# The last head's first maxima put into the first eight of its twelve expert tiles, with group 0's negative maxima made and sent before the last two tiles end

## What is computed

```python
x = L0_attn_hidden_states                      # 2 x 1024 x 256
xn = _layernorm(x)
x = x + attention(xn) + experts(xn)

# attention, per sequence and head
scores = q @ k.T * scale + slope * (pos_k - pos_q)     # causal, else -1e9
attn = softmax(scores, axis=-1)
out = (attn @ v) @ out_w.T + out_b

# experts
scores = sigmoid(x @ gate_w); selected = top_k(scores + expert_bias, 2)
routed += comb[:, e] * (silu(g) * u @ experts_down[e])  # for each expert e
shared = silu(x @ shared_gate_w) * (x @ shared_up_w) @ shared_down_w
```

## Time and profile before

| | |
|---|---|
| median of three runs | 511.94 us (509.26 to 513.58) |
| the profiled execution | 515.17 us, span 513.3 us |
| TensorE matmul busy | 449.6 us, 88% of the span |
| VectorE | 334.2 us, 65% |
| ScalarE | 249.0 us, 49% |
| GpSimd | 155.8 us, 30% |
| chain that ended last | TensorE 72%, VectorE 13%, DMA 7% |

### The profile page before, as it was taken

The page is one execution under the profiler, slowest core; times in us unless marked ns, Lnnn a source line. Parts: engine busy times, 40 slices in busy tenths (PEclk is TensorE's granted clock), DMA queues, the critical chain, the costliest instruction groups (busy, mean ns, idle before and its releaser), DMA issues.

```text
span 513.3 us, 8621 instructions
## 1 busy us (share of the span) xinstructions
PE 449.6 (88%) x2987; PEld 259.9 (51%) x2988; DVE 334.2 (65%) x621; ACT 249.0 (49%) x567; POOL 155.8 (30%) x178
## 2 busy tenths in 40 slices
PE   4597764498899999995998999999999999999996
PEld 3446652386576666673534444344444444433454
DVE  3869940365366666665786767867688586874667
ACT  2630520331333333331766667676676676766730
POOL 2380777201500000004888888840000101000000
PEclk9699795599999999997899999999999999999999
DMA  8797972379999984334116519162080000001103
GB/s 270 148 402 266 349 269 102 112 240 270 184 226 222 226 189 123 115 100 145 49 42 127 100 50 179 39 108 41 13 132 1 5 1 5 1 2 15 34 32 102
DMA packets 51484, 64.64 MB, mean 126 GB/s; under 512 B 13810, under 2 KB 44674, under 8 KB 49878
## 3 DMA queue, kind: packets, MB, share of 16 engines
q1 hardware_dynamic: 47046, 55.20, 41.8%
q0 software_dynamic: 3296, 8.52, 6.1%
q10 hardware_dynamic: 1104, 0.41, 0.3%
HBM read 37.47 MB, written 27.13 MB: 126 GB/s over the span
## 4 chain that ended last, share of the span: by engine, by line
PE 72%; DVE 13%; DMA 7%; issue 5%; SPq 2%; ACT 1%; DVEq 0%
PE ps L1277 12%; PE ps L1072 11%; PE ps L1251 10%; PE ps L1263 10%; PE ps L1176 9%; DVE mx L987 5%; PE ps L1192 5%; PE ps L1266 2%; PE ps L1252 2%; PE ps L1166 2%; DMA qs<-nr 2%; DMA x_in<-sorted_tokens 2%; DMA x_sb<-x 2%; PE ps L1205 2%; PE ps L1122 1%
## 5 line engine op out<-in xcount | busy, mean ns | idle before, releaser
L735 ACT ACTIVATE pt<-ps 128x512 f32<-128x512 f32 (+3 forms) x384 | 167.2, 491 | 83.7 <-PE ps L1266 47.7
L987 DVE TENSOR_REDUCE mx<-ps 128x1 f32<-128x384 f32 (+6 forms) x189 | 153.8, 863 | 55.8 <-PE ps L1252 53.2
L1277 PE MATMUL ps<-pt,vg 128*32 128x512 f32 (+3 forms) x768 | 71.9, 492 | 0.0
L592 POOL DMA_INDIRECT yg<-sorted_outputs,slot_i x32 | 32.7, 1020 | 109.5 <-DMA sorted_outputs<-y_out 101.0
L1263 PE MATMUL ps<-qs,ks 111*128 111x512 bf16 (+3 forms) x192 | 56.3, 333 | 4.1 <-DMA qs<-nr 3.3
L1176 PE MATMUL ps<-w_gu,hx 128*128 x192 | 54.2, 407 | 4.0 <-issue 3.3
L1263 PE MATMUL ps<-qk 111*128 111x512 bf16 (+3 forms) x192 | 54.6, 328 | 2.5 <-DMA qk<-nr 1.3
L1251 PE MATMUL ps<-qk 108*128 108x512 bf16 (+3 forms) x192 | 50.2, 328 | 2.8 <-DVE mx L987 2.4
L1266 PE MATMUL ps<-cbf 128*128 128x128 bf16 x256 | 52.6, 222 | 0.0
L1252 PE MATMUL ps<-cbf 128*128 128x128 bf16 x224 | 47.6, 225 | 0.0
L952 DVE COPY y_out<-ps 128x256 f32<-128x256 f32 x48 | 20.4, 424 | 37.7 <-PE ps L1192 37.6
(11 more groups left out here) (176 smaller groups left out, 680.1 us busy)
## 6 DMA issues: line engine op xcount, KB each, us to landing
sorted_tokens<-y_out SPq DMA_DIRECT2D x12, 512.0 KB, 5.0
qk_parts<-parts SPq DMA_DIRECT2D x16, 384.0 KB
x_in<-sorted_tokens SPq DMA_DIRECT2D x48, 128.0 KB, 4.0
sorted_outputs<-y_out SPq DMA_DIRECT2D x48, 128.0 KB, 2.1
qk<-qk_parts SPq DMA_DIRECT2D x8, 384.0 KB
w_gu<-e_gu SPq DMA_DIRECT2D x1, 2816.0 KB
x_sb<-x SPq DMA_DIRECT2D x4, 512.0 KB, 9.2
w_dn<-e_dn SPq DMA_DIRECT2D x1, 2048.0 KB, 8.3
```

The lines of the kernel that those rows point to most:

```text
L592: g_.indirect_dma_start(out=yg[:, n % 4, :], out_offset=None, in_=ysd, in_offset=bass.IndirectOffsetOnAxis(ap=slot_i[:, k, t:t + 1], axis= ...
L735: sc.activation(pt[:, s % 4, j, lo:CH], bank(n % 3)[:, lo:CH], ACT.Exp).then_inc(s_exp, 1)
L987: last = v.reduce_max(dst, src, axis=AX.X)
L1277: ins = te.matmul(ps[32 * j:32 * j + 32, OUT_BANK * CH + lo:(OUT_BANK + 1) * CH], vg[:, par, kb, j, :], pt[:, s % 4, j, lo:CH], start=kb = ...
```

## The change

The fourth head's eight maxima follow its tiles 0 to 7 (overall tiles 36 to 43) in place of 0, 2, 3, 5, 6, 8, 9 and 11. After its tile 9 (overall 45) TensorE transposes the maxima and VectorE makes the negative ones, and SyncE sends them after the store of tile 45, ahead of the stores of tiles 46 and 47. In the kernel before, all three steps come after tile 47. VectorE's helper functions also change place in the file, which moves line numbers alone. The waits added are those that the moved steps carry: TensorE's for the 32 maxima (s_ff) after tile 45, and SyncE's for the finished parts (s_n) ahead of store 46.

```diff
 FIRST_HEAD_AT = [NTH - QT + q for q in range(QT)]
+LAST_HEAD_AT = list(range(QT))
+FIRST_NEG_AT = QT + 1
...
             for k in range(NT - 8, NT):
                 store_tile(k, k % 4)
-            store_neg(0, 0)
+                if k == NT - NTH + FIRST_NEG_AT:
+                    store_neg(0, 0)
...
             def tile_steps(j, first, last):
...
                     tile_step(k + u, u % 4, NTH - u if last else NT, None if first and u < 4 else stored)
                     for q in range(QT):
-                        if (FIRST_HEAD_AT if first else FIRST_AT)[q] == u:
+                        if (FIRST_HEAD_AT if first else LAST_HEAD_AT if last else FIRST_AT)[q] == u:
                             first_maxima(j, q, j * QT + q)
+                    if last and u == FIRST_NEG_AT:
+                        negate(0, 0, first=True)
...
-            negate(0, 0, first=True)
             for p in range(EARLY):
                 maxima(1, 1, p)
...
                     for q in range(QT):
-                        if (FIRST_HEAD_AT if first else FIRST_AT)[q] == u:
+                        if (FIRST_HEAD_AT if first else LAST_HEAD_AT if last else FIRST_AT)[q] == u:
                             first_scores(j, q, j * QT + q, first)
+                    if last and u == FIRST_NEG_AT:
+                        pe.wait_ge(s_ff, HG * QT)
+                        te.transpose(bank(6, P, HG * QT), mx[:, 0, :], ident[:, :]).then_inc(s_fr, 1)
...
             tile_steps(HG - 1, False, True)
-            pe.wait_ge(s_ff, HG * QT)
-            te.transpose(bank(6, P, HG * QT), mx[:, 0, :], ident[:, :]).then_inc(s_fr, 1)
             pe.wait_ge(s_yo, NT)
             pe.wait_ge(s_ff, HG * QT + 1)
```

More of the change, by code:

```diff
@@ L937, in _, with negate @@
                 add_shared(n)
+            def negate(g, par, first=False):
+                ready, freed, n = (s_fr, s_ff, HG * QT) if first else (s_mxr, s_mxf, g * NP - 1)
+                dve.wait_ge(ready, n + 1)
+                src = bank(6, P, HG * QT)
+                v.tensor_scalar(nr[:, par, 0, :], src, -1.0, None, ALU.mult).then_inc(s_nstep, 1)
+                dve.wait_ge(s_nstep, g * 2 + 1)
+                v.scalar_tensor_tensor(nrf[:, par, :], src, -1.0, nr[:, par, 0, :], ALU.mult,
+                                       ALU.subtract).then_inc(freed, 1)
+                dve.wait_ge(freed, n + 1 if first else MX_CREDIT + n + 1)
+                v.tensor_copy(nr[:, par, 1, :], nrf[:, par, :]).then_inc(s_nstep, 1)
+                dve.wait_ge(s_nstep, g * 2 + 2)
+                v.tensor_tensor(nr[:, par, 2, :], nrf[:, par, :], nr[:, par, 1, :], ALU.subtract).then_inc(s_n, 1)
             def tile_hidden(k, w):
@@ L988, in maxima @@
                 last.then_inc(s_mxf, 1)
[L990 to L1002, removed]
             def beside(g, par, ahead):
```

## The result

The changed kernel takes 1.0058 times as long as the kernel before, with a 95% interval of 1.0037 to 1.0079. That is 3.0 us more (1.9 to 4.1); the medians of eight runs are 516.30 and 512.03 us, 4.3 us apart, and the text goes by the ratio. The forecast was 0.35% slower, 1.8 us, in a range of 509.7 to 516.5 us; the measured median lies inside it, 0.2 us from its upper end. The interval is clear of no change, which the prediction had not expected of so small a difference.

The account below looks back on a forecast made before the run. TensorE ran at full clock in most slices, except around the 7.6 us tail before group 0, mostly latency. Group 3's start (-0.2) and half clock (+2.0) gave +1.8 us: 517.0 profiled, 513.7 on the median, range 509.7 to 516.5.

Parts of the forecast that it names:

- The tiles: Tiles 36 to 45, sized from the first head's tiles with maxima blocks: tile 45 starts at 229.18 us, 0.65 late.
- The negative maxima: Between tile 45 and group 0: parts ready at about 233.1 us in place of 236.62, group 0 3.6 us earlier.
- The landing: From the first issue of the three DMAs to TensorE's start of group 0: 4.81 us, unchanged.
- The clock at group 0: TensorE's clock no longer falls to half at group 0's start, as the tail is filled: 2.03 us back.
- SyncE's order: The three DMAs go ahead of the last two stores, so GpSimd's first gather moves 1.52 us later, to 237.93.
- The wait at group 3: TensorE, 5.6 us ahead, waits 5.4 us for GpSimd's v copy ending at 338.60; 0.2 us of gain is left.
- GpSimd's own stretch: GpSimd's work from the first gather to the end of group 3's v copy: 100.67 us, taken as unchanged.
- The half clock behind the wait: TensorE's work after the wait at group 3 starts at half clock: 2.0 us lost, between 0 and 4.1.
- The sum: Whole kernel: -0.2 us at group 3's start and +2.0 of half clock make +1.8 us, 0.35% slower.
- The v copy does not bind: Rival, chance 0.12: GpSimd has more slack at group 3, the whole 5.6 us stays, 506.3 us, 1.1% faster.
- Binds, but the clock does not fall: Rival, chance 0.18: TensorE waits for the v copy at group 3 without half clock; only -0.2 us, 511.7 us.
- A long cold start: Rival, chance 0.08: half clock lasts much longer after the wait at group 3, 20 us giving +7.6, 519.5 us.

Follow-up runs that it names:

- the maxima alone: Changed kernel with transposition, negation and sending put back behind tile 47, only the fourth head's maxima kept early; 0.9980 (0.9955 to 1.0005) of the kernel before.

## Why the prediction was right, point by point

**The tiles.** Foreseen from tile 36 to tile 45: 18.43 us. Measured: 225.67 - 207.10 = 18.57. The first head's rows were the right stand-in.

**The negative maxima.** Foreseen 22.35 us from tile 36 to ready parts, measured 229.57 - 207.10 = 22.47. The landing was mis-sized: 4.81 us from the first issue was taken from the kernel before, and it took 232.89 - 229.60 = 3.29. With the parts 0.1 later, that put group 0 a further 1.4 us ahead, all of which went into the wait. The 4.81 was not a chance of one execution: in the kernel before with GpSimd 4 us longer it took 4.76, and with the maxima alone 4.73; with the early v copy in the kernel before it took 3.97 (issue 233.72, group 0 at 237.69). The six kernels that send early took 3.14 to 3.85. So the way from issue to group 0 mostly became shorter with the change, where the prediction had it unchanged; why, no run shows.

**The clock at group 0.** Foreseen +2.0 back, measured 8.25 - 6.23 = 2.0. That it came out to the tenth is luck: in four of the six executions with the early sending the clock fell here all the same, though none of these kernels alters TensorE's work up to there (GpSimd 4 us longer: 7.49 us). The mean of the six is 6.81 us and that of the three of the kernel before 7.91, a gain of 1.1. In the changed kernel's time this hardly counts, since the wait at group 3 takes up what group 0 gains or loses.

**SyncE's order.** Foreseen 1.52 us later for the first gather, measured 27.87 - 25.66 = 2.21. Of the 0.7 us between, 0.4 is the issue of the last two stores: 1.06 us together (0.5 each), where 0.32 to 0.36 each had been put in, taken from the last store of the kernel before. The other 0.3 is the three rows: ready 0.1 later, and 1.99 us to issue in place of 1.84.

**The wait at group 3.** Foreseen 5.4 us, measured 7.55. The 2.15 us more are four terms, to within 0.1: group 0 began 1.4 us earlier than thought, TensorE's way from there to group 3 took 94.55 us in place of 333.2 - 237.9 = 95.3, the gather came 0.7 us later, and against these GpSimd's own stretch was 0.75 us shorter. Foreseen start 0.2 us earlier than before, measured 0.19 from tile 36. This agreement is luck, since two errors met: the gather came 0.7 us later than thought, and GpSimd's own stretch took 99.92 us in place of 100.67, since two waits of 0.7 us for gathered rows fell to one of 0.55.

**The half clock behind the wait.** Foreseen 2.0 us, measured 1.73, and shown as a cost of its own by the kernel that kept TensorE busy (13.51 us back to 11.78). The rule of the Trainium skill (TensorE: Matmul & The Clock Gate, section on oscillation) holds here: the trace has 7.55 us of idle time and then 4.44 us at clock 0.50.

**The sum.** +1.8 foreseen, and from the two profiled executions, both from tile 36 on: 511.7 - 207.10 = 304.6 against 513.3 - 210.75 = 302.55, +2.05. The ratio says +3.0 (1.9 to 4.1). The rest, if it is not noise, may lie in the kernel before: its profiled execution reached group 3 1.4 us later (128.08) than the one with the early v copy (126.65), which does the same work up to there and runs in the same time. Against that one the sum is 1.24 + 1.73 = 3.0. The kernel that keeps TensorE busy points the same way: without the half clock it is still 1.5 us (0.4 to 2.6) slower than the kernel before, where the prediction has -0.2. I took one execution's distance to group 3 as the kernel's, and its slack of 1.75 us with it. That the loss at group 3 is a microsecond more is worked out from one execution of each kernel, not shown.

**The rivals.** "The v copy does not bind" is refuted by the 7.55 us; what it would have given, 1.1% faster, is what the variant with the early copy gave (1.0%). "Binds, but the clock does not fall" is refuted for the changed kernel by the 4.44 us at 0.50; the kernel with TensorE kept busy is that case made, though at +1.5 us and not at the -0.2 that the rival gave. A long cold start did not come: the clock was back after 4.44 us.

## What to carry to other kernels

When a stage is shortened, look down the program for every place where another engine joins, and read its slack there: what reaches the stage behind it can't be more than the slack there (1.75 us here by one execution, less what the change itself adds to that engine's start, 1.5 foreseen and 2.2 measured). Read the slack in more than one execution: here one had 1.75 us and another about 1. What is moved ahead in an in-order queue pushes back what it passes; ask who waits for that, even 100 us later. Each idle wait of TensorE at group 3 cost more than its length, 1.1 to 2.2 us more, because the work behind it ran at half clock, and the remedy may be one line elsewhere: moving a 0.6 us copy turned +0.6% into -1.0%.

## What was not expected of the hardware

- From the first issue of the same three small DMAs to TensorE's start of group 0 it took 3.14 to 3.85 us in the six kernels that send early, and 3.97 to 4.81 in the four that send behind tile 47 and negate there. In the two that negate early and send behind the last stores it took 3.15 and 4.15.
- With TensorE's instructions ahead of it the same, the clock at group 0 stayed at 1.00 in two profiled executions and fell in four.
- Two copies of 480 KB from DRAM to DRAM, issued 0.34 us before an indirect gather, held its rows up for 1.76 us; issued 2.2 us before it, or 1.27 us behind it, they did not (one execution each).
- Of 4.44 us at half clock 1.73 were lost, and of 5.23 us 2.0, so 39% of the time, not half, although TensorE was busy all through.
